# Cross-attention and rank-six self-attention on one core: second attention started inside the loop, additions shared out, unused TensorE products

## The chip, the core and the metric

The kernel runs on one core of a Trainium2 chip. The metric is the device time of one execution in microseconds (us). TensorE (PE) does the matrix products and the transposes, VectorE (DVE), ScalarE (ACT) and GpSimd (POOL) work on 128 partitions, SyncE (SP) issues all DMAs. SBUF tiles are named in the code; PSUM has eight banks of 128 x 512 fp32.

## What is computed

Two layers follow each other. B = 32 batches, N = 256 tokens, D = 256 features.

```python
# layer 0, 16 heads of 16 features; only the attention of batch 0 is used, and it is added to every batch
q, k, v = tgt @ Wq.T, memory @ Wk.T, memory @ Wv.T
x = tgt + softmax(q k^T / 4) v [batch 0]
# layer 1, per batch; ctx are the keys and values, x the queries
norm_X   = layernorm(ctx, norm1);  norm_F = layernorm(x, norm2)
attended = softmax(norm_F norm_X^T / 16) norm_X
h        = gelu(attended @ fc1_w.T + fc1_b)          # 4 hidden values per token
cross    = h @ fc2_w.T + fc2_b
norm_c   = layernorm(cross, norm3)
self_att = softmax(norm_c norm_c^T / 16) norm_c      # "second attention"
out      = norm_F + gamma2 * (cross + gamma1 * self_att)
```

Since `cross` is an affine function of 4 hidden values, `norm_c` has rank 6. The second attention therefore works on 6 numbers per token (`u` on one side, `uK` on the other), each cut into bf16 pieces so that the products keep fp32 accuracy.

## The kernel before

All engines run programs written out by hand, in which semaphores order the work between them; each engine works strictly in the order of its own program. There are four parts.

**First stage (layer 0, batch 0).** TensorE projects q, k and v (L822, L834). The 16 heads go through as eight pairs, `p` = 0 to 7: scores (L865), maxima on DVE (`hmax`, L380), exp on ACT (L718), transposes of the weights (L881) into banks 5 and 6, their copies to `PT` by ACT (bank 5, L724) and DVE (bank 6, L386), and after every other pair the product with v (L894). ACT's order per pair is four exps, then the copy of the pair ahead; TensorE's transposes wait for both copies (`pt0_ok`). DVE also takes statistics of ctx in between (L351), at `p` = 6 it clears the padding of `sU` (L400), and at `p` = 7 makes pieces of the output operand. The result is `tgt2`.

**Filling.** `tgt2` is added to `x`: batches 0 and 1 on DVE (L468), all others on POOL (`add`, L615). Then come statistics (L351), the root on POOL (L622), the normalising (DVE `normal`, L371 for x, POOL L635 for ctx), transposes on TensorE (L852) and their evacuation by ACT to `XT` and `Fall` (L735, L738), with weight and bias applied.

**The loop, b = 0 to 35.** TensorE per batch: the transposes of a later pair (L852), the scores (L915), and the transposes of the exps of the batch ahead (L923); once per four batches (a "quad", `q`) the hidden projection and its way back (L935, L943), the product of the weights with it (L953) and its way back (L961). DVE takes the maxima (`maximum`, L488), statistics and normals of later batches, and copies `vT` (L514) and `oTq` (L522); ACT does exps (L762) and the copies to `PT` (L756). The tables LATE and NEXT say behind which step DVE does which part of the small-rank algebra (`algebra(g, part)`, g = 0 for the first half of the batches, 1 for the second): h, gelu on ACT (`hidden`), the norm by Newton steps, `u`, `uK`, the pieces in `sU`. POOL makes the other side's pieces (`right`).

**Second attention and output, after the loop.** Sixteen pairs of batches, `p` = 0 to 15: transposes of `sU` into bank 4 (`turn`, L1001), their copy to `sT` (ACT for even, DVE for odd `p`), scores (L1012, into banks 0 and 1 or 2 and 3), maxima on DVE (`maxima`, L535), turned by TensorE (L1023), copied by ACT (`nm2T`, L781) and added to the scores by a product (`shift`, L1031), exp on ACT (L787). Per quad: the product with `u` (`attend`, L1044), a copy by DVE (`collected`, L548), the turn back (`back`, L1053), the division on DVE (`returned`, L553 to L558), pieces on POOL (`output_cuts`, L681 to L688), their transposes (`output_turn`, L1063, bank 4 too), ACT's copy to `cT` (L794). Per pair n: the output product (`output(n)`, L1073, banks 6 and 7) and the addition of `Fall` on DVE (`finish`, L564), after which SP stores the pair. `output(n)` comes five steps behind pair n and waits for `finish(n-1)`.

```python
        def output(n):
            pe.wait_ge(cT_ok, n // 2 + 1)
            if n >= 1:
                pe.wait_ge(fin_ok, n)
```

Of the kernel before, what the change touches and what calls it, by code (L numbers as in the profile page):

```python
# [28 lines left out]
P = 128  # L29
B = 32  # L30
# [17 lines left out]
LATE = {26: (0,), 29: (1,), 30: (2,), 31: (3,), 32: (4,), 33: (5,)}  # L48
NEXT = {0: (0,), 2: (1,), 3: (2, 3), 4: (4,), 5: (5,)}
# [21 lines left out]
def build(nc, x, ctx, x0t, c0t, wqt, wkt, wvt, params, out):  # L71
# [121 lines left out]
    h_ok, co_ok, sC_ok = sem("h_ok"), sem("co_ok"), sem("sC_ok")  # L193
# [44 lines left out]

    TURNS = [(p, 0) for p in range(EARLY)] + [(p, 1) for p in range(EARLY)] \
# [15 lines left out]
    def _(sp):  # L255
# [18 lines left out]
    def _(dve):  # L274
# [10 lines left out]
        def left_cuts(v, left, to, w):  # L285

            link(dve.tensor_copy(slots(to, w, SLOTS_L[0]), repeated(v, 3)))
            link(dve.tensor_tensor(left, v, to[:, :, 0:w], ALU.subtract))
            link(dve.tensor_copy(slots(to, w, SLOTS_L[1]), repeated(left, 2)))
            link(dve.tensor_tensor(to[:, :, 5 * w:6 * w], left, to[:, :, 3 * w:4 * w], ALU.subtract))  # L290

# [8 lines left out]

        dve.wait_ge(par_in, 16)
# [32 lines left out]
        output_operand(1)  # L334
# [5 lines left out]
        link(dve.tensor_copy(K[:, :], bank[5][:, 64:64 + U * U]), "QK")  # L340
        stats = [0]

        def statistics(b, side):
# [3 lines left out]
            elif b < 2:  # L347
                dve.wait_ge(y_first, b + 1)
            else:
                dve.wait_ge(y_ok, b - 1)  # L350
# [23 lines left out]
        for p in range(NHP + 1):  # L374
# [12 lines left out]
            if p < NHP:  # L387
# [32 lines left out]

        def products(v, m, n):

            w = big[:, 0:GROUP * n * n].rearrange("p (t j i) -> p t j i", t=GROUP, j=n)
            link(dve.tensor_tensor(w, v.unsqueeze(2).to_broadcast([P, GROUP, n, n]),
                                   m.rearrange("p (j i) -> p j i", j=n).unsqueeze(1).to_broadcast([P, GROUP, n, n]),
                                   ALU.mult))
            return w
# [6 lines left out]
        def algebra(g, part):  # L434
# [9 lines left out]
            elif part == 1:  # L444
                dve.wait_ge(gelu_ok, g + 1)
                dve.wait_ge(zero_ok, 8)
                link(dve.tensor_reduce(w5, products(ha[:, G, :], Q[:, :], H + 1), AX.X, ALU.add))
                link(dve.tensor_tensor(w5, w5, ha[:, G, :], ALU.mult))
                link(dve.tensor_reduce(v, w5, AX.X, ALU.add))
            elif part == 2:  # L450
# [4 lines left out]
            elif part == 3:  # L455
# [3 lines left out]
            elif part == 4:  # L459
# [692 lines left out]
```

## Time and profile before

| | |
|---|---|
| median of 3 runs (lowest to highest) | 263.16 us (262.43 to 263.74) |
| the profiled execution | 262.2 us, span 260.4 us |
| busy in the span | PE 213.0, DVE 207.4, ACT 140.9, POOL 125.4 us |
| granted TensorE clock, mean | 0.854 of full |

The page gives the busy share of each engine in forty slices of 6.5 us, the granted clock of TensorE in tenths, and groups of instructions by line. A timeline lists the instructions of one engine in order: start, length, engine, line, operation, count, and in brackets the idle time before them with what ended it. The chain of waits follows the last instruction back through whatever released it.

### The profile page before, as it was taken

What the parts mean: (1) busy time and instruction counts of PE and PEld (TensorE: products, weight loads), DVE (VectorE), ACT (ScalarE), POOL (GpSimd) and SP (SyncE); (2) the same over time, 40 slices, a digit from 0 to 9 for tenths busy, and PEclk for the clock granted to TensorE, in tenths of its full rate; (3) what the DMA queues carried; (4) which work ended last, traced back from release to release, by engine and by line L of the source; (5) the groups of instructions that cost most, each with busy time, mean ns of one, the idle gap of its engine ahead of it and who ended that gap; (6) DMA issues with size and microseconds to landing.
All of it is one profiled execution on the core that took longest, in us unless ns stands there. A gap on an engine that the chain in (4) does not pass through costs nothing.

```text
span 260.4 us, 4676 instructions
## 1 busy us (share of the span) xinstructions
PE 213.0 (82%) x1614; PEld 143.4 (55%) x1614; DVE 207.4 (80%) x413; ACT 140.9 (54%) x260; POOL 125.4 (48%) x186
## 2 busy tenths in 40 slices
PE   3989868289999999999999999963786568888731
PEld 3856535267778778796988789632222223333210
DVE  5678886999999989888998953886569958988663
ACT  1066764216677778586776778840564335454300
POOL 6000087677999979999697840041003512222220
PEclk9999999659999999999999999985555557777865
DMA  5980000044444425355450000000000024333556
GB/s 185 363 302 3 1 1 3 0 161 161 165 161 142 144 95 156 114 164 162 159 166 0 4 0 3 0 0 3 1 0 1 0 83 162 141 144 125 204 198 242
DMA packets 14711, 26.80 MB, mean 103 GB/s; under 512 B 1760, under 2 KB 1760, under 8 KB 14688
## 3 DMA queue, kind: packets, MB, share of 16 engines
q1 hardware_dynamic: 14688, 26.50, 29.2%
q8 instruction: 13, 0.21, 0.3%
q14 instruction: 10, 0.08, 0.1%
HBM read 18.11 MB, written 8.39 MB: 102 GB/s over the span
## 4 chain that ended last, share of the span: by engine, by line
PE 59%; DVE 24%; ACT 6%; issue 6%; POOL 2%; DMA 1%; SPq 0%; POOLq 0%; DVEq 0%; ACTq 0%
PE psum L915 17%; PE psum L852 8%; PE psum L923 5%; PE psum L1044 4%; DVE xN L371 4%; DVE nm L535 3%; DVE bn L351 3%; PE psum L953 3%; PE psum L822 2%; PE psum L935 2%; PE psum L1012 2%; DVE Fall L564 2%; PE psum L1073 2%; PE psum L865 2%; PE psum L881 2%
## 5 line engine op out<-in xcount | busy, mean ns | idle before, releaser
L915 PE MATMUL psum<-XT,Fall 128*128 128x256 f32 x256 | 62.6, 388 | 1.1 <-ACT Fall L738 1.1
L915 PEld LDWEIGHTS psum<-XT,Fall 128*128 128x128 f32 x256 | 47.2, 195 | 7.1 <-ACT Fall L738 1.7
L615 POOL TENSOR_TENSOR xN<-xN,tgt 128x512 f32<-128x512 f32 x30 | 39.1, 1306 | 1.5 <-DVE tgt L415 1.5
L635 POOL TENSOR_SCALAR cN<-cN,nmean,rstd 128x256 f32<-128x256 f32 x64 | 36.4, 579 | 2.4 <-POOL rstd L622 2.3
L371 DVE TENSOR_SCALAR xN<-xN,bn,rstd 128x256 f32<-128x256 f32 x64 | 34.8, 586 | 1.1 <-POOL rstd L622 1.1
L756 ACT ACTIVATE PT<-psum 128x512 f32<-128x512 f32 x32 | 19.1, 598 | 28.6 <-PE psum L923 28.6
L488 DVE TENSOR_REDUCE nmax<-psum 128x2 f32<-128x512 f32 x32 | 21.9, 684 | 12.6 <-PE psum L915 12.4
L622 POOL TENSOR_TENSOR rstd<-vps,minus_half 128x8 f32<-128x8 f32 (+1 forms) x16 | 24.8, 1549 | 13.8 <-DVE vps L362 13.8
L762 ACT ACTIVATE E<-psum,nmax 128x256 f32<-128x256 f32 x64 | 26.7, 473 | 8.3 <-DVE nmax L488 8.2
L681 POOL CAST sC<-co 128x160 bf16<-128x160 f32 x8 | 2.5, 317 | 53.9 <-DVE co L558 53.9
L738 ACT ACTIVATE Fall<-psum,par 128x512 f32<-128x512 f32 x32 | 23.4, 792 | 4.8 <-PE psum L852 4.7
L564 DVE TENSOR_TENSOR Fall<-psum,Fall 128x1024 f32<-128x1024 f32 x16 | 19.5, 1221 | 7.6 <-PE psum L1073 7.6
L735 ACT ACTIVATE XT<-psum,b1s,w1s 128x512 f32<-128x512 f32 x32 | 23.0, 788 | 3.7 <-PE psum L852 3.7
L535 DVE TENSOR_REDUCE nm<-psum 128x4 bf16<-128x1024 f32 x16 | 19.5, 1218 | 4.5 <-PE psum L1012 4.3
L351 DVE BATCH_NORM_STATS2 bn<-cN 128x6 f32<-128x512 f32 x32 | 22.2, 693 | 0.0
L852 PE MATMUL psum<-ident,xN 128*128 128x128 f32 x128 | 18.2, 289 | 4.7 <-DVE xN L371 4.7
L351 DVE BATCH_NORM_STATS2 bn<-xN 128x6 f32<-128x512 f32 x32 | 21.9, 685 | 0.0
L923 PE MATMUL psum<-ident,E 128*128 128x128 f32 x128 | 20.2, 280 | 1.6 <-ACT E L762 1.6
L787 ACT ACTIVATE PT<-psum 128x1024 f32<-128x1024 f32 x16 | 16.4, 1022 | 9.2 <-PE psum L1031 9.1
L923 PEld LDWEIGHTS psum<-ident,E 128*128 128x128 f32 x128 | 14.3, 141 | 9.6 <-issue 6.5
L852 PEld LDWEIGHTS psum<-ident,xN 128*128 128x128 f32 x128 | 15.7, 150 | 5.5 <-issue 5.1
L852 PE MATMUL psum<-ident,cN 128*128 128x128 f32 x128 | 17.1, 274 | 0.1
(156 smaller groups left out, 337.0 us busy)
## 6 DMA issues: line engine op xcount, KB each, us to landing
cN<-ctx SPq DMA_DIRECT2D x32, 256.0 KB, 2.9
xN<-x SPq DMA_DIRECT2D x32, 256.0 KB, 4.1
out<-Fall SPq DMA_DIRECT2D x32, 256.0 KB, 2.3
x0T<-x0t SPq DMA_DIRECT2D x1, 256.0 KB, 2.7
wqT<-wqt SPq DMA_DIRECT2D x1, 256.0 KB, 3.3
c0T<-c0t SPq DMA_DIRECT2D x1, 256.0 KB, 4.0
wkT<-wkt SPq DMA_DIRECT2D x1, 256.0 KB, 5.0
wvT<-wvt SPq DMA_DIRECT2D x1, 256.0 KB, 5.2
```

Source lines behind the costliest of these rows:

```text
L351: dve.bn_stats(bn[:, (b // 2) % 4, side, b % 2, :], src[:, b % SLOTS, :].rearrange("p (t d) -> p d t", t=NT)).then_inc(st_ok, 1)
L371: dve.tensor_scalar(own, own, stat(p, 1, m, t, 1), root_of(p, 1, m, t), ALU.subtract, ALU.mult)\
L535: dve.tensor_reduce(nm2[:, p % 2, :, 0:NT], scored(p).rearrange("p (m t k) -> p m t k", m=2, t=NT), AX.X, ALU.max, negate=True).then_inc(m ...
L564: dve.tensor_tensor(own, psum[:, 6 * 512:8 * 512], own, ALU.add).then_inc(fin_ok, 1)
L615: pool.tensor_tensor(xN[:, b % SLOTS, :], xN[:, b % SLOTS, :], tgt2[:, :, :].rearrange("p t d -> p (t d)"), ALU.add).then_inc(y_ok, 1)
L622: pool.tensor_tensor(rstd[:, p % 4, sides, :].rearrange("p s k -> p (s k)"), vps[:, p % 4, sides, :].rearrange("p s k -> p (s k)"), minus_ ...
L635: pool.tensor_scalar(own, own, nmean[:, p % 4, NT * m + t:NT * m + t + 1], root_of(p, 0, m, t), ALU.add, ALU.mult)\
L738: act.activation(Fall[:, 2 * p:2 * p + 2, c, :], tiles(own), ACT.Identity, bias=c_("b2", c), scale=c_("w2", c)).then_inc(evac_ok, 1)
L762: act.activation(E[:, b % 2, t * N:(t + 1) * N], bank[SBANK1[b % 3]][:, t * N:(t + 1) * N], ACT.Exp, bias=nmax[:, b % 2, t:t + 1]).then_in ...
L852: last = pe.transpose(bank[TBANK[n % 3]][:, m * N + t * P:m * N + (t + 1) * P], z[:, (2 * p + m) % SLOTS, t * D + c * P:t * D + (c + 1) * ...
L915: last = pe.matmul(bank[SBANK1[b % 3]][:, t * N:(t + 1) * N], Fall[:, b, c, t * P:(t + 1) * P], XT[:, p % 4, c, m * N:(m + 1) * N], start= ...
L923: last = pe.transpose(bank[SBANK1[b % 3]][:, k * N + t * P:k * N + (t + 1) * P], E[:, b % 2, t * N + k * P:t * N + (k + 1) * P], ident[:, :])
```

## The change

- **First stage.** ACT copies the pair ahead between the two halves of its exps, and TensorE's transposes wait only for the copy of their own bank. The clearing of `sU` moves to DVE's first instructions, the second part of the output operand out to loop step 18, and the first part of it behind the copies of Q and K. DVE adds `tgt2` to batches 2 and 3, too, and POOL starts its additions at batch 4, behind DVE's first four normals.
- **Loop.** `vT` and `oTq` are copied by ACT. The algebra of the first half is cut into nine parts and done at steps 20 to 29 (gelu at 21). The transposes and scores of the second attention's first pair are issued at b = 30 and 31, inside the loop; the last quad's `apply` and `apply_back` follow inside step p = 0 of the second attention.
- **Second attention.** All `sT` copies are done by ACT. For n = 1, 3, ... 13 (ASIDE) ACT copies the output from PSUM to the old space of `XT` behind the exp, and POOL adds `Fall` there. `output(13)` and `output(15)` use banks that the scores have left.
- **Unused products.** `keep_busy(n, b)` issues n products of the identity with itself into bank b, which nothing reads: 7 at the start, 11 behind the transposes of ctx, 4 and 3 at the change from the loop, 5 per step p below 5 and 2 per step after.

The diff, cut to its core:

```diff
-LATE = {26: (0,), 29: (1,), 30: (2,), 31: (3,), 32: (4,), 33: (5,)}
-NEXT = {0: (0,), 2: (1,), 3: (2, 3), 4: (4,), 5: (5,)}
+LATE = {20: (0,), 22: (1,), 23: (2,), 24: (3,), 25: (4,), 26: (5,), 27: (6,), 28: (7,), 29: (8,)}
+NEXT = {0: (0,), 2: (1, 2), 3: (3, 4), 4: (5, 6), 5: (7, 8)}
+ASIDE = tuple(range(1, 14, 2))
...
@@ sync @@
-        for b in range(B):
-            sp.wait_ge(fin_ok, b // 2 + 1)
+        for n, b in ((n, b) for n in STORED for b in (2 * n, 2 * n + 1)):
+            if n in ASIDE:
+                sp.wait_ge(added_ok, ASIDE.index(n) + 1)
+            else:
+                sp.wait_ge(fin_ok, own_adds(n) + 1)
...
@@ vector @@
+        for side in range(2):
+            dve.memset(sU[:, side, :, SU:SLOT], 0.0).then_inc(pads_ok, 1)
...
-                if p == 2 * EARLY:
-                    for side in range(2):
-                        dve.memset(sU[:, side, :, SU:SLOT], 0.0).then_inc(zero_ok, 1)
-                elif p > 2 * EARLY:
-                    output_operand(2)
...
-        statistics(2, 1)
+        add(2)
+        add(3)
         normal(0)
         normal(1)
+        statistics(2, 1)
...
-                dve.tensor_copy(vT[:, :], bank[6][:, 0:N]).then_inc(vT_ok, 1)
...
-                    dve.tensor_copy(oTq[:, :], bank[7][:, 0:N]).then_inc(oTq_ok, 1)
...
-        def turned(p):
...
-            dve.tensor_copy(sT[:, 1, :], bank[4][:, 0:NT * P].bitcast(BF16)).then_inc(sT_ok[1], 1)
...
         maxima(0)
-        turned(1)
+        saved(QUADS - 1)
         for p in range(2 * QUADS + 5):
...
-            if p >= 5:
+            if p >= 5 and p - 5 not in ASIDE:
                 finish(p - 5)
...
@@ gpsimd @@
+        def add_aside(n):
+            pool.wait_ge(aside_ok, ASIDE.index(n) + 1)
+            pool.tensor_tensor(pair(n), aside(n), pair(n), ALU.add).then_inc(added_ok, 1)
...
                 output_cuts((p - 3) // 2)
+            if p - 5 in ASIDE:
+                add_aside(p - 5)
...
@@ scalar @@
+                if m == 0 and p >= 1:
+                    act.wait_ge(p0_mm, 2 * p - 1)
...
+                    act.activation(PT[:, 2 * ((p - 1) % 3), :], bank[5][:, :], ACT.Copy).then_inc(pt0_ok[0], 1)
...
+        def set_aside(n):
+            act.wait_ge(f_mm, n + 1)
...
+            act.activation(aside(n), results(n), ACT.Copy).then_inc(aside_ok, 1)
...
-            if p % 2 == 0 and p + 2 < PAIRS:
+            if p + 2 < PAIRS:
                 turned(p + 2)
             if p < PAIRS:
                 weights(p)
+            if p - 5 in ASIDE:
+                set_aside(p - 5)
...
@@ tensor @@
+        def keep_busy(n, b):
+            for _ in range(n):
+                pe.matmul(bank[b][:, 0:P], ident[:, :], ident[:, :], start=True, stop=True)
+
+        pe.wait_ge(consts, 4)
+        keep_busy(7, 4)
...
-                if p >= 2:
-                    pe.wait_ge(pt0_ok[0], p - 1)
-                    pe.wait_ge(pt0_ok[1], p - 1)
                 for m in range(2):
+                    if p >= 2:
+                        pe.wait_ge(pt0_ok[m], p - 1)
...
+        keep_busy(11, 7)
...
+            if b == 31:
+                scores(0)
+            if b == B:
+                pe.wait_ge(V1_ok, QUADS)
+                keep_busy(4, 6)
+            if b >= 1:
+                weights_turned(b - 1)
...
+            if b == 30:
+                turn(0)
+            if b == 31:
+                turn(1)
         for p in range(2 * QUADS + 5):
             if p < PAIRS:
                 maxima_turn(p)
+            if p == 0:
+                keep_busy(3, 6)
+                apply(QUADS - 1)
             if p + 1 < PAIRS:
                 scores(p + 1)
+            if p == 0:
+                apply_back(QUADS - 1)
             if p + 2 < PAIRS:
                 turn(p + 2)
             if p < PAIRS:
                 shift(p)
+                keep_busy(5 if p < 5 else 2, 5)
```

TensorE's order from the last scores but one of the loop (L915, after the change L981) to the second attention, before and after. `stR` is the output operand, `E` the exps, `V` the hidden values, `sU` and `sT` the pieces of the second attention, `nm` its maxima.

```order
L915 MATMUL psum<-XT,Fall 128x256 x4
L961 MATMUL psum<-ident,oTq 128x128 x2
L923 MATMUL psum<-ident,E 128x128 x8
L953 MATMUL psum<-PT,V 5x256 x8
L961 MATMUL psum<-ident,oTq 128x128 x2
L1001 MATMUL psum<-identb,sU 128x128 x4
L1012 MATMUL psum<-sT 128x256 x4
L1001 MATMUL psum<-identb,sU 128x128 x4
L1023 MATMUL psum<-identb,nm 64x128
```

```order
L1048 MATMUL psum<-identb,sU 128x128 x4
L981 MATMUL psum<-XT,Fall 128x256 x4
L1027 MATMUL psum<-ident,oTq 128x128 x2
L1063 MATMUL psum<-sT 128x256 x4
L989 MATMUL psum<-ident,E 128x128 x4
L1048 MATMUL psum<-identb,sU 128x128 x4
L873 MATMUL psum<-ident 128x128 x4
L989 MATMUL psum<-ident,E 128x128 x4
L1074 MATMUL psum<-identb,nm 64x128
L873 MATMUL psum<-ident 128x128 x3
L1019 MATMUL psum<-PT,V 5x256 x8
```

The first `turn` (L1001, now L1048) has moved ahead of the last scores, the second attention's first scores (L1012, now L1063) directly behind them, and the last quad's product (L953, now L1019) behind the first turned maxima.

ACT's order in two steps p of the second attention, before and after (`PT` with 1024 columns is the exp of a pair, `XT` with 1024 columns the output set aside).

```order
L781 ACTIVATE nm2T<-psum 64x128
L775 ACTIVATE sT<-psum 128x512
L787 ACTIVATE PT<-psum 128x1024
L794 ACTIVATE cT<-psum 128x512
L781 ACTIVATE nm2T<-psum 64x128
L787 ACTIVATE PT<-psum 128x1024
```

```order
L830 ACTIVATE nm2T<-psum 64x128
L800 ACTIVATE sT<-psum 128x512
L838 ACTIVATE PT<-psum 128x1024
L851 ACTIVATE XT<-psum 128x1024
L845 ACTIVATE cT<-psum 128x512
L830 ACTIVATE nm2T<-psum 64x128
L800 ACTIVATE sT<-psum 128x512
L838 ACTIVATE PT<-psum 128x1024
```

Between the exp of an even step and the copy to `cT` stands the output set aside (L851), and odd steps have an `sT` copy.

## Rows read from the trace of the kernel before

**Rows 1.** The page: busy time by engine, and TensorE's granted clock by slice.

```profile
PE 213.0 (82%) x1614; PEld 143.4 (55%) x1614; DVE 207.4 (80%) x413; ACT 140.9 (54%) x260; POOL 125.4 (48%) x186
...
PEclk9999999659999999999999999985555557777865
```

**Rows 2.** Stretches: busy time of PE, PEld, DVE, ACT, POOL (last: PE alone), PEclk, DMA share, GB/s.

```profile
62.00:170.00 108.00, 107.48 (x825) 87.09 (x825) 92.40 (x201) 79.15 (x148) 80.04 (x88) 1.00 0.31 101
...
214.24:221.24 7.00, 6.25 (x58) 2.54 (x56) 5.89 (x9) 3.67 (x7) 1.50 (x5) 0.74 0.40 151
...
176.00:214.00 38.00, 24.56 (x173) 0.50 0.04 15
```

**Rows 3.** Timeline of TensorE, the first two projections.

```profile
4.92 3.78 PE L822 MATMUL psum<-x0T,wqT 128*128 128x256 f32 x8 [0.47 <-DMA wqT<-wqt]
8.50 2.88 PE L822 MATMUL psum<-c0T,wkT 128*128 128x256 f32 x8
```

**Rows 4.** Chain of waits in the first stage: start, length, what.

```profile
24.23 1.09 PE psum L865 x8
...
28.17 1.09 PE psum L881 x8
...
30.27 1.09 PE psum L865 x8
...
33.55 0.81 DVE sU L400
...
37.44 0.50 ACT PT L724
37.98 1.10 PE psum L881 x8
```

**Rows 5.** Filling: all x normals (least, median, most ns); their chain; TensorE's timeline.

```profile
L371 DVE TENSOR_SCALAR xN<-xN,bn,rstd x64: 396/404/1412, 48.7 to 157.8; 128x256 f32<-128x256 f32 x64
...
48.71 2.31 DVE xN L371 x4
...
52.97 3.27 DVE xN L371 x4
...
50.52 2.09 PE L852 MATMUL psum<-ident,xN 128*128 128x128 f32 x8 [4.69 <-DVE xN L371]
```

**Rows 6.** Timeline of ACT in the loop, around the gelu.

```profile
161.77 1.28 ACT L743 ACT_TABLE_LOAD   x1
```

**Rows 7.** Timelines of TensorE and DVE from the last loop scores to the first maxima.

```profile
168.49 1.95 PE L915 MATMUL psum<-XT,Fall 128*128 128x256 f32 x8
...
173.85 1.47 PE L953 MATMUL psum<-PT,V 128*5 128x256 f32 x16 [0.69 <-ACT PT L756]
178.32 0.69 PE L961 MATMUL psum<-ident,oTq 128*128 128x128 f32 x2 [2.99 <-DVE oTq L522]
...
180.77 1.23 DVE L535 TENSOR_REDUCE nm<-psum 128x4 bf16<-128x1024 f32 x1 [1.53 <-PE psum L1012]
```

**Rows 8.** Second attention: timelines of DVE, TensorE and ACT, then groups (busy, mean ns).

```profile
210.21 1.22 DVE L535 TENSOR_REDUCE nm<-psum 128x4 bf16<-128x1024 f32 x1
...
217.29 0.22 PE L1023 MATMUL psum<-identb,nm 128*64 128x128 bf16 x1 [0.74 <-DVE OB L553]
...
238.46 0.22 PE L1023 MATMUL psum<-identb,nm 128*64 128x128 bf16 x1 [1.03 <-DVE OB L553]
...
220.81 0.60 ACT L794 ACTIVATE cT<-psum 128x512 bf16<-128x512 bf16 x1 [1.02 <-PE psum L1063]
...
L787 ACT ACTIVATE PT<-psum 128x1024 f32<-128x1024 f32 x16 | 16.4, 1022 | 9.2 <-PE psum L1031 9.1
L564 DVE TENSOR_TENSOR Fall<-psum,Fall 128x1024 f32<-128x1024 f32 x16 | 19.5, 1221 | 7.6 <-PE psum L1073 7.6
L615 POOL TENSOR_TENSOR xN<-xN,tgt 128x512 f32<-128x512 f32 x30 | 39.1, 1306 | 1.5 <-DVE tgt L415 1.5
```

**Rows 9.** Timeline of DVE: the last addition.

```profile
256.02 1.23 DVE L564 TENSOR_TENSOR Fall<-psum,Fall 128x1024 f32<-128x1024 f32 x1 [0.80 <-PE psum L1073]
```

More of the change, by code:

```diff
@@ L237, in score_bank, with own_adds, result, results @@
         return bank[2 * (1 - p % 2) + m]
+    def own_adds(n):
+        return sum(i not in ASIDE for i in range(n))
+    STORED = tuple(range(13)) + (14, 13, 15)
+    def result(n):
+        return {13: (2, 3), 15: (0, 1)}.get(n, (6, 7))
+    def results(n):
+        a, _ = result(n)
+        return psum[:, 512 * a:512 * (a + 2)]
+    def aside(n):
+        return XT[:, (n // 2) % 2, :, :].rearrange("p c n -> p (c n)")
+    def pair(n):
+        return Fall[:, 2 * n:2 * n + 2, :, :].rearrange("p b c n -> p (b c n)")
     TURNS = [(p, 0) for p in range(EARLY)] + [(p, 1) for p in range(EARLY)] \
@@ L458, in algebra, with add @@
                 link(dve.tensor_tensor(u[:, G, 0:H + 1], ha[:, G, :], spread(y, H + 1), ALU.mult), ("u", g))
[L459 to L460 removed]
+            elif part == 5:
+                products(u[:, G, :], K[:, :], U)
+            elif part == 6:
+                link(dve.tensor_reduce(uK[:, G, :], produced(U), AX.X, ALU.add))
+            elif part == 7:
+                left_cut(uK[:, G, :], cut[:, G, 0:U], sU[:, 0, G, :], U)
             else:
[L462 removed]
+                left_rest(cut[:, G, 0:U], sU[:, 0, G, :], U)
                 ALG["left", g] = count[0]
[L465 removed]
+        def add(b):
             dve.wait_ge(tgt2_ok, 2 * NT)
@@ L499, in values, with saved @@
             dve.tensor_copy(V1[:, q % 2, :, :, 0:H], by_batch(bank[6][:, 0:N], H)).then_inc(V1_ok, 1)
-        for b in range(B + 4):
+        def saved(q):
+            dve.wait_ge(ob_mm, q + 1)
+            dve.tensor_copy(OA[:, q, :, :, :], by_batch(bank[7][:, 0:N], H + 1)).then_inc(o_saved, 1)
+        for b in range(B):
             k, m, q = b // 2, b % 2, b // 4
@@ L707, in _ @@
         for p in range(NHP + 1):
-            if p == 6:
-                act.wait_ge(o0_mm, NHP // 4)
-                act.activation(oT[:, 0, :], bank[0][:, :], ACT.Copy).then_inc(oT_ok[0], 1)
-            if p < NHP:
-                for m in range(2):
+            for m in range(2):
+                if p < NHP:
                     act.wait_ge(max0_ok, 2 * p + m + 1)
@@ L774, in turned @@
                 act.wait_ge(s2_mm, p - 1)
-            act.activation(sT[:, 0, :], bank[4][:, 0:NT * P].bitcast(BF16), ACT.Copy).then_inc(sT_ok[0], 1)
+            act.activation(sT[:, p % 2, :], bank[4][:, 0:NT * P].bitcast(BF16), ACT.Copy).then_inc(sT_ok[p % 2], 1)
+        for p in range(EARLY):
+            evacuate(p, 0)
+        evacuate(0, 1)
+        for b in range(B):
+            k, m, q = b // 2, b % 2, b // 4
+            if k + 1 < PAIRS and (m == 1 or k + 1 >= EARLY):
+                evacuate(k + 1, m)
+            if b >= 1:
+                weights_copied(b - 1)
+            exponentials(b)
+            if b % 4 == 1:
+                turned_values(q)
+            if b % 4 == 2 and q >= 1:
+                applied(q - 1)
+            if b == 21:
+                hidden(0)
+            if b == 29:
+                act.wait_ge(r_mm, 1)
+                act.activation(RT[:, :], bank[4][:, 0:DC * P // 2].bitcast(BF16), ACT.Copy).then_inc(rt_ok, 1)
+            if b == 30:
+                turned(0)
+        weights_copied(B - 1)
+        turned(1)
         def maxima_turned(p):
```

214 lines of the change are left out of this document (107 added, 107 removed).

## The prediction

> **What bounds the kernel now.** The page comes first [rows 1]: TensorE is busy for 213.0 of 260.4 us and DVE for 207.4, so no single engine bounds the whole, and TensorE's granted clock sags at the filling and in the last third. The stretches say which part has which limit [rows 2]. From 62 to 170 us TensorE is busy for 107.48 of 108 us at full clock: the loop is bound by TensorE, nothing can be taken from it by helping another engine, and any lateness of another engine adds to it. In one quad of the second attention (214.24 to 221.24) TensorE has 6.25 and DVE 5.89 of 7.00 us at a mean clock of 0.74: both are close to the limit, and TensorE's share shrinks if its clock rises. From 176 to 214 the clock is 0.50, that is 1.2 of 2.4 GHz, with TensorE busy for 24.56 of 38 us. Then the chain of waits and the timelines show the changes between parts: the start [rows 3], the first stage [rows 4], the filling [rows 5] and the 10.5 us between the end of the loop's last scores and the first maxima of the second attention [rows 7].
>
> All sums are made against the profiled execution, 262.2 us (span 260.4 and 1.8 around it), which lies 1.0 below the median of 263.16; the forecast adds that 1.0 back.
>
> **1. The start: -1.4.** The first projection takes 3.78 us for eight records and the second 2.88 [rows 3]; at full clock eight such records take some 1.9 (as L915 does in [rows 7], 1.95), so TensorE reached 2.4 GHz only about 4.5 us after the first projection began. Seven unused products start as soon as the identity is there. Each is worth half an L915 product, 0.22 us at full and 0.43 at half clock, so they fill about 3 us up to the first projection, which may start some 0.5 later. Nothing lost to half clock would be -2.8, less the 0.5 is -2.3; nothing gained and the late start is +0.5. I take -1.4, nearer the first, since the warm-up begins 3 us sooner.
>
> **2. First stage: -4.2.** Two head pairs take 6.0 us now, from scores to scores (24.23 to 30.27), and the chain runs through ACT's copy, then the transposes [rows 4]. With the copy between the halves of the exps, the transposes of bank 5 start 0.7 to 0.8 us earlier, before the second half, and TensorE becomes the limit: scores twice, transposes twice (1.1 each, less overlap) and the product with v (1.0) are 5.2. That is -0.8 in each of two such turns, -1.6. At the end the two memsets (0.81 and as much again) lie on the chain and leave it, -1.7; at the last pair the copy (0.50 at 37.44) stood behind both exp halves, and its transposes (37.98) now start one half and the copy earlier, -0.9. Together -4.2. The bounds are -1.7 (the memsets alone) and -6. The moved memsets cost nothing: they run before the parameters arrive. The pieces of the output operand now stand between the copies of Q and K and the first maxima, where DVE waits for the first scores anyway; without that cover they cost 0.8.
>
> **3. Filling: -2.0.** DVE is the chain here. Four normals take 2.31 and 3.27 us while POOL adds beside them, and one alone takes 0.40, four 1.6 [rows 5]. POOL's additions now wait for the first four: -0.7 there, and about -1.0 at the next four, which meet one addition instead of two. DVE's own two further additions (0.7 each when alone) run while POOL takes the root, where DVE has nothing else to do. With the `vT` copy moved to ACT (-0.3) this gives -2.0. The eleven products keep TensorE going through part of its 4.69 us of waiting; if its clock stays up, the first x transposes take 0.9 instead of 2.09 [rows 5] and the first scores 1.9 less, but DVE is not there earlier, so I book nothing for it. Bounds: 0 (POOL is simply late elsewhere) and -4. The contention itself shows in the least and the most of one normal, 396 and 1412 ns [rows 5]. The Trainium skill says in "SBUF — State Buffer" (§ SBUF: two separate sides) that DVE and GpSimd share one port pair, held for a whole instruction; by that rule the 3.27 would fall to 1.6 only where no addition starts between normals, and the trace agrees in kind.
>
> **4. Loop: +1.3.** TensorE has no slack, so what is moved in costs. The turn of the first pair adds 0.35. DVE has 15.6 us of idle time in 108 [rows 2], 0.5 per batch, and gains 0.2 by the two copies that go to ACT. Steps 20 to 25 bring 1.0 to 1.9 us each of algebra, while it still takes statistics. I let it fall behind by at most 2.5 us where the exp allows it about 1.2 to 2.2, so TensorE waits some 0.6. The gelu's two table loads at 21 (1.28 each [rows 6]) hold ACT by 2.9 us where evacuations still follow: 0.4. ACT is at 79 of 108 us, and two copies more per quad do not bound it. Bounds 0.35 and +4.
>
> **5. From the loop to the seventh `maxima`: -8.5.** Count from the end of the last loop scores, S. Now S is at 170.3 (last scores from 168.49, [rows 7]); the first maxima start 10.5 later, because `oTq` stands behind the algebra on DVE and the turn behind both [rows 7]; `maxima(7)` starts at 210.21, S + 39.9 [rows 8]. After: scores follow S directly (0.8), maxima(0) until 2.0; the last exps, four unused products, their transposes until 3.4; ACT's `PT` copy until 4.0; the last `apply` 4.3 to 5.3; scores of pair 1, `apply_back`, `saved` on DVE, so maxima(1) from 6.2. The lead of 9.7 shrinks there to 6.1. Then exp(0) ends at 8.0, maxima(2) runs from 8.5, maxima(3) from 10.8; the gelu's two table loads put exp(2) at 15. From 15 to 31 DVE is the limit with the algebra of the second half (about 9 us), maxima 4 to 6 and one `finish`; without its two `sT` copies and the stall behind the half-clock `attend` it reaches maxima(7) at S + 31.4. The difference is 8.5. The unused products, five per step, lie before work that waits for DVE. Bounds -5 and -11.
>
> **6. From there to step 14: -1.1.** Now 210.21 to 238.46 [rows 8], 28.2 us. DVE loses a `finish` (1.22, [rows 8]) and an `sT` copy per quad and would need only 4.5 us. But a new chain appears. ACT sets the output aside only when TensorE has ended an even step, 3.35 us of work at full clock; the copy takes 1.02 as an exp of equal size does, `cT` follows (0.60), and only then may the next `turn` overwrite bank 4 and `nm2T` be copied, whereupon turn, shift, two unused products, `back` and `output` take another 1.9. That is 3.35 + 1.6 + 1.9 = 6.9 per quad against 7.0 now. What remains is the start: 27.1 instead of 28.2. This hangs on full clock, and a range follows below. Bounds without the clock: -7 (period 5.5, TensorE's own work) and +1.
>
> **7. The end: +2.0.** From `mt` of step 14 (L1023, 238.46) to the end of the last addition (257.25) [rows 8, 9] are 18.8 us. After, POOL adds pair 11 before it makes the last pieces. A POOL addition of 512 columns takes 1.31 us [rows 8], of 1024 I take 2.5; it ends 2 us after the pieces could start. The last pieces, `cT` behind the set-aside of pair 13, and two additions in a row on free banks bring 19.75, +1.0; three pairs are stored together at the end, +1.0. The Trainium skill ("GPSIMD Engine Reference", § 3.1) measures 4.5 us for a GpSimd addition of 2048 fp32 and advises DVE for such work; that speaks against this part, and an estimate from it is 2.25 for 1024, 0.25 less than by the rows.
>
> **Sum.** -1.4 - 4.2 - 2.0 + 1.3 - 8.5 - 1.1 + 2.0 = -13.9, so 248.3 for an execution like the profiled one and **249.2** for the median.
>
> **The clock.** At 214 to 242 us it goes back and forth between 1.2 and 2.4 GHz (mean 0.74, [rows 2]), and it falls after stretches in which TensorE waited no longer than 0.74 to 1.03 us at a time [rows 8]. After, TensorE waits 1.15 of 6.9 us, with 0.9 us of full-width products more. I take it that those keep it up. "TensorE: Matmul & The Clock Gate" of the Trainium skill (§ HAM oscillation) names only long idle gaps between bursts as what throttles the array; by that rule the clock would stay up, and the sum above stands as it is. The rows disagree with it, and by them the next case is open.
>
> **Rivals.**
> - **The clock keeps swinging in the second attention.** With 5.2 us of TensorE work on the chain of a quad and about half the time at 1.2 GHz, T = 1.65 + 5.2 + T/4, near 8.5 to 9. At 8.5 against 6.9 over 3.9 quads that is +6.3: **255.5**. For it: [rows 2]. Against it: more and wider products.
> - **ACT and POOL take the additions without a hand-over cost**, since the copy falls into the time before the exp: the quad falls to 5.5, TensorE's own work, 1.4 less by 3.9 quads: **243.7**. For it: DVE's 5.89 of 7.00 is then gone. Against it: the order on ACT.
> - **The loop cannot feed the early start.** DVE's algebra or ACT's table loads make TensorE wait for 4 to 5 us around steps 21 to 26: **253.5**.
> - **The unused products do not lift the clock, which stays at 1.2 GHz as from 176 to 214 us [rows 2], and they then cost**: the 5.25 us of TensorE's work per quad become about 8.8 (a part of it does not follow the clock), with 1.6 that is 10.4; +3.5 by 3.9 is +13.7, and five products of 0.43 instead of 0.22 in each of three early steps on the chain are another +3.3: **266**, slower than before. It decides from a loss of 14 on, that is, when practically no stretch is at full clock. For it: 38 us at 0.50 with TensorE busy 65%. Against it: at 6.25 of 7.00 us busy [rows 2] it came back up each time.
>
> **How the numbers follow.** Forecast 0.59; swinging clock 0.17; no hand-over cost 0.15; loop late 0.05; low clock throughout 0.04. The forecast's own bounds (start, filling and stage each off by 1 to 2, mostly independent) make it 245 to 253. From 243 to 256 all cases but the last are in, less the tails of two, about 0.8. A change under 0.5%, 1.3 us, is about what can't be told from none. Faster 0.95, same 0.01, slower 0.04.
>
> **What would show it.** Right: `tgt2` ready near 38 us; L915's successor at 3.7 us per batch with waits under 1.5 us in all; first maxima 0.8 us behind the last scores and the second about 5 later; a quad near 6.9 us with a wait of about 1.1 us of TensorE for `cT`; PEclk 9 in the last third; `output_cuts(7)` behind POOL's addition. Wrong: quads near 5.5 or 8.5; PEclk of 5 to 7 behind 165 us; DVE maxima late in the loop from step 22; a first stage that still takes 6 us per two pairs.

## The result and the profile after

The changed kernel takes **269.92 us** (median of 4 runs, 267.93 to 270.31) against 263.45 (262.43 to 263.82) for the kernel before: ratio 1.0237, 95% interval 1.0176 to 1.0297. It is slower by 6.5 us. The forecast was 249.2, with a range of 243 to 256, so the result lies outside it, and on the other side of no change. The profiled execution takes 270.31 us, with a span of 268.5. Medians here and below are of all executions of a kernel, while ratios and their intervals leave out those more than 1.5% above its fastest, all of them at a lower granted clock (two of the four of e4, one of e11 with 258.64 us, among others).

The page of the changed kernel (busy time by engine, TensorE's granted clock in forty slices of 6.7 us, two of its groups):

```profile
span 268.5 us, 4992 instructions
...
PE 232.3 (87%) x1758; PEld 161.4 (60%) x1758; DVE 190.3 (71%) x384; ACT 155.4 (58%) x291; POOL 141.0 (53%) x191
...
PEclk9999999999999999999999999999855575575555
...
L711 POOL TENSOR_TENSOR Fall<-XT,Fall 128x1024 f32<-128x1024 f32 x7 | 16.5, 2354 | 31.2 <-ACT XT L851 31.2
...
L873 PE MATMUL psum<-ident 128*128 128x128 f32 x144 | 27.4, 343 | 1.9 <-POOL ident L608 1.9
```

Against [rows 1], DVE has 17 us less to do and TensorE 19 us more. The clock now holds through the filling and far into the second attention, and then stays at 1.2 GHz for most of the last 75 us. The unused products (L873) alone are busy for 27.4 us.

Where the time went, by four marks of the program (all from the timelines; the quad is (step 14 - step 8) / 3, and the tail runs from step 14 to the end of the span):

| us | before | after | difference | forecast |
|---|---|---|---|---|
| last loop scores start | 168.49 | 165.68 | -2.8 | -6.3 |
| from there to `maxima(7)` | 41.72 | 33.89 | -7.8 | -8.5 |
| from there to step 14 (TensorE's turn of the maxima) | 28.25 | 40.17 | **+11.9** | -1.1 |
| tail | 21.94 | 28.76 | **+6.8** | +2.0 |
| span | 260.4 | 268.5 | +8.1 | -13.9 |

At `maxima(7)` (199.57 against 210.21 of [rows 8]) the changed kernel led by 10.6 us. All of that was lost before step 14, and the tail then added to it. Stretches of TensorE in the changed kernel (busy time, records, granted clock, DMA):

```profile
186.00:192.00 6.00, 3.81 (x43) 1.00 0.00 1
192.00:198.00 6.00, 4.85 (x28) 0.51 0.00 0
198.00:204.00 6.00, 4.36 (x32) 0.50 0.25 90
204.00:210.00 6.00, 5.09 (x33) 0.50 0.14 52
210.00:216.00 6.00, 6.00 (x44) 0.50 0.33 123
216.00:222.00 6.00, 4.86 (x39) 0.78 0.30 107
222.00:228.00 6.00, 5.09 (x40) 0.50 0.19 72
```

The clock falls at 192 us, behind a wait of 2.11 us for DVE's algebra. One quad of it in TensorE's timeline:

```profile
212.71 1.89 PE L1095 MATMUL psum<-PT,u 128*6 128x256 f32 x16
214.53 0.61 PE L1114 MATMUL psum<-identb,sC 128*128 128x128 bf16 x4
215.07 0.61 PE L1130 MATMUL psum<-cT,RT 60*128 60x256 bf16 x4
215.61 0.32 PE L1074 MATMUL psum<-identb,nm 128*64 128x128 bf16 x1
215.86 0.45 PE L1063 MATMUL psum<-sT 36*128 36x256 bf16 x4
217.38 0.38 PE L1048 MATMUL psum<-identb,sU 128*128 128x128 bf16 x4 [1.07 <-ACT cT L845]
217.69 0.39 PE L1082 MATMUL psum<-nm2T,sel 2*128 2x256 bf16 x4
218.01 0.71 PE L873 MATMUL psum<-ident 128*128 128x128 f32 x4
...
219.48 0.61 PE L1063 MATMUL psum<-sT 36*128 36x256 bf16 x4
220.02 0.61 PE L1048 MATMUL psum<-identb,sU 128*128 128x128 bf16 x4
220.56 0.61 PE L1082 MATMUL psum<-nm2T,sel 2*128 2x256 bf16 x4
221.10 1.22 PE L873 MATMUL psum<-ident 128*128 128x128 f32 x4
```

and what ACT does meanwhile:

```profile
211.67 1.02 ACT L838 ACTIVATE PT<-psum 128x1024 f32<-128x1024 f32 x1
215.72 1.02 ACT L851 ACTIVATE XT<-psum 128x1024 f32<-128x1024 f32 x1 [3.03 <-PE psum L1130]
216.64 0.59 ACT L845 ACTIVATE cT<-psum 128x512 bf16<-128x512 bf16 x1
```

The same shapes take 0.39 us at one level of the clock and 0.61 at the other. TensorE is busy for 6.00 of 6.00 us from 210 to 216, the clock comes back, TensorE waits 1.07 us for `cT`, and 2.1 us behind that wait it is at 1.2 GHz again. The source of `cT` (L1114) ends at 215.14, but its copy starts at 216.64: the copy set aside stands ahead of it in ACT's program and needs `output` (L1130), which TensorE does after L1114. So `cT` comes 1.5 us late, and ACT stood idle for 3.03 us before.

The chain of waits from 180 to 262 us shows who pays (shares of that stretch):

```profile
by line: PE psum L873 15.8%; PE psum L1095 12.4%; issue 11.4%; PE psum L1130 8.3%; PE psum L1082 7.3%; PE psum L1048 5.7%; PE psum L1114 4.8%; PE psum L1063 4.0%; ACT cT L845 3.6%; DVE nm L564 3.0%; POOL Fall L711 2.9%; PE psum L1104 2.6%; 
```

The unused products are the largest entry, 15.8% of 82 us, that is 13 us.

### The profile page after: what moved, and what is told of

Its sections match the earlier page's. It is cut to its first block, busy times and chain, and to the rows that moved or that the text cites. A ratio compares the mean times of both kernels' runs of the same rounds, so it can differ in the third digit from the quotient of the medians.

```text
span 268.5 us, 4992 instructions
## 1 busy us (share of the span) xinstructions
PE 232.3 (87%) x1758; PEld 161.4 (60%) x1758; DVE 190.3 (71%) x384; ACT 155.4 (58%) x291; POOL 141.0 (53%) x191
## 4 chain that ended last, share of the span: by engine, by line
PE 60%; DVE 21%; issue 7%; ACT 6%; POOL 3%; ACTq 1%; DVEq 0%; POOLq 0%
PE psum L981 14%; PE psum L873 7%; PE psum L918 6%; DVE bn L381 5%; DVE xN L401 5%; PE psum L989 5%; PE psum L1095 4%; PE psum L1019 3%; PE psum L1130 3%; PE psum L1082 2%; PE psum L1048 2%; PE psum L931 2%; DVE nmax L524 2%; PE psum L1001 2%; PE psum L888 2%
## 5 line engine op out<-in xcount | busy, mean ns | idle before, releaser
L981 PE MATMUL psum<-XT,Fall 128*128 128x256 f32 x256 | 60.9, 381 | 1.8 <-ACT Fall L763 1.8
L981 PEld LDWEIGHTS psum<-XT,Fall 128*128 128x128 f32 x256 | 46.1, 190 | 7.2 <-ACT Fall L763 2.2
L656 POOL TENSOR_SCALAR cN<-cN,nmean,rstd 128x256 f32<-128x256 f32 x64 | 38.8, 618 | 2.4 <-POOL rstd L643 2.3
L636 POOL TENSOR_TENSOR xN<-xN,tgt 128x512 f32<-128x512 f32 x28 | 35.7, 1278 | 1.6 <-DVE xN L401 1.6
L401 DVE TENSOR_SCALAR xN<-xN,bn,rstd 128x256 f32<-128x256 f32 x64 | 33.9, 573 | 0.7 <-POOL rstd L643 0.7
L711 POOL TENSOR_TENSOR Fall<-XT,Fall 128x1024 f32<-128x1024 f32 x7 | 16.5, 2354 | 31.2 <-ACT XT L851 31.2
L873 PE MATMUL psum<-ident 128*128 128x128 f32 x144 | 27.4, 343 | 1.9 <-POOL ident L608 1.9
L873 PEld LDWEIGHTS psum<-ident 128*128 128x128 f32 x144 | 22.7, 237 | 7.1 <-issue 5.2
L851 ACT ACTIVATE XT<-psum 128x1024 f32<-128x1024 f32 x7 | 7.2, 1024 | 24.3 <-PE psum L1130 24.3
L989 PE MATMUL psum<-ident,E 128*128 128x128 f32 x128 | 20.2, 280 | 0.3 <-ACT E L793 0.2
L918 PE MATMUL psum<-ident,xN 128*128 128x128 f32 x128 | 17.1, 274 | 2.6 <-DVE xN L401 2.3
L989 PEld LDWEIGHTS psum<-ident,E 128*128 128x128 f32 x128 | 14.3, 141 | 8.3 <-issue 6.3
```

The costliest lines, as they stand in the source:

```text
L401: dve.tensor_scalar(own, own, stat(p, 1, m, t, 1), root_of(p, 1, m, t), ALU.subtract, ALU.mult)\
L636: pool.tensor_tensor(xN[:, b % SLOTS, :], xN[:, b % SLOTS, :], tgt2[:, :, :].rearrange("p t d -> p (t d)"), ALU.add).then_inc(y_ok, 1)
L656: pool.tensor_scalar(own, own, nmean[:, p % 4, NT * m + t:NT * m + t + 1], root_of(p, 0, m, t), ALU.add, ALU.mult)\
L873: pe.matmul(bank[b][:, 0:P], ident[:, :], ident[:, :], start=True, stop=True)
L918: last = pe.transpose(bank[TBANK[n % 3]][:, m * N + t * P:m * N + (t + 1) * P], z[:, (2 * p + m) % SLOTS, t * D + c * P:t * D + (c + 1) * ...
L981: last = pe.matmul(bank[SBANK1[b % 3]][:, t * N:(t + 1) * N], Fall[:, b, c, t * P:(t + 1) * P], XT[:, p % 4, c, m * N:(m + 1) * N], start= ...
```

## The experiments

Theory A: the copy set aside ahead of `cT` makes TensorE wait; the waits bring the clock down and keep it there, and at that clock nearly all of TensorE's work is on the chain. Rival B: the unused products themselves are the cost. Rival C: they hold the clock up and are worth having. Rival D: the `sT` copies, all on ACT now, make the wait. "The kernel before" was run beside each group; its medians were 262.62, 263.45 and 263.63. What every profile showed, in us:

| kernel | median | clock | `maxima(7)` at | quad | tail |
|---|---|---|---|---|---|
| before | 263.45 | 0.854 | 210.21 | 7.06 | 21.94 |
| after | 269.92 | 0.870 | 199.57 | 10.02 | 28.76 |
| e1 no step products | 260.22 | 0.856 | 198.42 | 8.37 | 26.74 |
| e2 no aside | 247.93 | 0.951 | 199.08 | 6.15 | 20.37 |
| e3 `cT` first | 253.39 | 0.939 | 198.60 | 7.07 | 24.03 |
| e4 neither | 248.64 | 0.910 | 198.09 | 6.05 | 20.51 |
| e5 five everywhere | 269.75 | 0.934 | 198.49 | 9.52 | 27.6 |
| e6 e2, more products | 251.55 | 0.949 | 200.51 | 6.13 | 20.65 |
| e7 before + products | 269.93 | 0.876 | 216.20 | 6.46 | 23.15 |
| e8 e3, pieces first | 251.39 | 0.955 | 198.41 | 6.56 | 23.33 |
| e9 e2, algebra earlier | **244.03** | 0.964 | 197.31 | 6.13 | 20.3 |
| e10 e9, few products | 245.75 | 0.928 | 197.91 | 6.13 | 20.03 |
| e11 e2, none at the start | 248.81 | 0.936 | 200.30 | 6.13 | 20.33 |
| e12 e2, filling as before | 249.56 | 0.932 | 200.88 | 6.15 | 20.33 |

### Products and additions, each alone and together

e1 takes the products out of the steps, e2 the additions off ACT and POOL, e4 does both, e3 only exchanges two calls:

```diff
 e1, e4:
-                keep_busy(5 if p < 5 else 2, 5)
 e2, e4:
-ASIDE = tuple(range(1, 14, 2))
+ASIDE = ()
-    STORED = tuple(range(13)) + (14, 13, 15)
+    STORED = tuple(range(16))
 e3, ACT's program:
-            if p - 5 in ASIDE:
-                set_aside(p - 5)
             if p == 1:
                 hidden(1)
             if p % 2 == 0 and p >= 4:
                 output_turned((p - 4) // 2)
+            if p - 5 in ASIDE:
+                set_aside(p - 5)
```

> The changed kernel without the unused products of the second attention's steps (5, then 2 per step); those at the start, behind the transposes of ctx and at the change from the loop stay. Theory A (ACT's copy of the output ahead of cT makes TensorE wait, the waits lower the clock, the products cannot lift it): quads of 9 to 10 us still at 1.2 GHz, time 263 to 267, that is 3 to 7 less than the changed kernel's 269.9, since at half clock two products (about 1.1 us a pair of steps) and the five of each early step lie on the chain. Rival B (the products themselves are the cost): quads near 7, time 255 to 259. Rival C (the products do hold the clock up in part): no faster, 270 to 274, with a granted clock lower than now.

> The changed kernel with all additions on DVE as before and the pairs stored in order; everything else of the change stays, the unused products too. Theory A (the copy set aside on ACT between the exp and cT stretches the quad and so lowers the clock): quads of 7 to 7.5 us at a swinging clock, the lead of 10 us at the first turn of the second half is kept, and the end is near 19 us again: time 252 to 258. Rival B (the unused products lie on the chain at half clock): quads of 8 to 9, 261 to 266. Rival D (all sT copies on ACT make the wait): quads still over 10, time 268 to 271.

> The changed kernel with one thing moved: ACT copies cT ahead of the output that it sets aside, in every even step. Theory A: cT comes 1.0 us earlier, TensorE's wait of 0.9 to 1.1 us for it in each quad goes, quads fall from 10.4 to 9.4 at least, 5 quads: time 263 to 266, and 255 to 258 if the clock comes back. Rival B (products) or D (sT copies): 269 to 271, since the wait for cT is then only a sign.

> Both of the first two edits: all additions on DVE, no unused products in the steps of the second attention. Theory A: as without the copies set aside, 252 to 257, the products then lie in waits and cost under 1 us or hold the clock. Rival B: 250 to 254, at least 5 less than with the products. Rival C (products hold the clock): 3 or more longer than with the products.

Measured, as ratios to the kernel before: e1 0.9936 (0.9902 to 0.9971), e2 0.9477 (0.9402 to 0.9553), e3 0.9682 (0.9618 to 0.9746), e4 0.9412 (0.9305 to 0.9519).

- **e3 decides for A.** One exchange of calls on ACT, with no work removed, is worth 16.5 us (269.92 to 253.39). Before the run I put it at 4 to 7, or 12 to 15 if the clock comes back. It comes back, and the gain lies just above that range. Page and a quad of e3:

```profile
PEclk9999999799999999999999999999998589799955
```

```profile
206.76:213.30 6.54, 5.90 (x64) 3.11 (x65) 4.81 (x8) 4.96 (x8) 3.86 (x7) 1.00 0.43 160
```

```profile
209.94 0.60 ACT L845 ACTIVATE cT<-psum 128x512 bf16<-128x512 bf16 x1 [0.76 <-PE psum L1114]
210.44 1.02 ACT L851 ACTIVATE XT<-psum 128x1024 f32<-128x1024 f32 x1
211.34 0.26 ACT L830 ACTIVATE nm2T<-psum 64x128 bf16<-64x128 bf16 x1
```

The copy of `cT` starts right behind L1114 (209.51, 0.40 long), not 1.5 us later. TensorE's longest wait in the quad falls from 1.07 to 0.58 us (now for `nm2T`), and the quad is 6.54 us long. At full clock the quad of the changed kernel would be some 6.8 us (an estimate from e5, below), so the wait itself is a small part of the difference to 10.02 and the clock is the rest.

- **e2** comes out 4 us below A's 252 to 258. It has quads of 6.12 us at full clock, with TensorE busy for 5.82 and DVE for 5.56 (stretch 210.44 to 216.56):

```profile
210.44:216.56 6.12, 5.82 (x66) 3.10 (x65) 5.56 (x8) 4.09 (x8) 1.51 (x5) 1.00 0.47 173
```

All 16 additions on DVE are thus no bound, and D falls, since the `sT` copies are still all on ACT. The early start of the second attention keeps its lead of 11 us. The clock of e2 falls too, around TensorE's waits of 2.10 and 1.72 us for DVE's algebra (which end at 191.92 and 196.02), but here it is back at 204.5 us and stays for the rest of the quads:

```profile
PEclk9999999889999999999999999999999858999965
```

- **The products** cost 9.7 us where the copy is set aside (e1, between A's 263 to 267 and B's 255 to 259), and nothing that can be told where it is not (e2 and e4 differ by 0.7; the executions of e4 run from 245.47 to 250.80, those of e2 from 247.56 to 248.30). B is therefore half right: they cost as long as the clock is low. C falls for these steps: without the products the quads of e4 are as short (6.05) at a lower mean clock. That two products per step take back what the full clock gives is argued from these two quads, not shown by itself. Both e2 and e4 lie below every range that I gave for them.

### Can more products bring the clock back?

```diff
 e5, after with:
-                keep_busy(5 if p < 5 else 2, 5)
+                keep_busy(5, 5)
 e6, e2 with:
+                keep_busy({5: 10, 6: 9}.get(p, 5 if p < 5 else 2), 5)
 e7, before with, behind shift(p):
+                keep_busy(5 if p < 5 else 2, 5)
 e8, e3 with, in POOL's program:
-            if p % 2 == 1 and 3 <= p < 2 * QUADS + 3:
+            if p % 2 == 1 and 3 <= p < 2 * QUADS + 1:
                 output_cuts((p - 3) // 2)
+            if p == 2 * QUADS:
+                output_cuts(QUADS - 1)
             if p - 5 in ASIDE:
                 add_aside(p - 5)
```

> The changed kernel with five unused products in every step of the second attention, not two behind the fifth. Theory A (TensorE's wait for cT pins the clock at 1.2 GHz, and no product stands in that wait, since each has its place behind the shift): six products more per quad at 0.55 us each at half clock are up to 3.3 us a quad, 5.5 quads: 280 to 288. Rival C (more products would lift the clock): quads near 7.5, time 252 to 260.

> The kernel with all additions on DVE (247.9 us) with ten instead of two unused products... in step 5 five more and in step 6 seven more than there, placed before the waits of 2.1 and 1.7 us for DVE's algebra, so that TensorE does not stand still there; everything else as in that kernel. Theory A (such waits throw the clock down, here from 196 to 204 us): granted clock full up to 199 us and time 245 to 248. If the clock falls all the same, behind the wait of 2.3 us for the turn, or the products lie on the chain: 248 to 251.

> The kernel before with one thing added: the unused products of the steps of the second attention (five per step below 5, two per step after). Theory A (products lift the clock only where they stand in TensorE's waits; before, it waits 0.74 to 1.03 us at a time for DVE): the clock of 176 to 214 us rises in part, the last third swings; 258 to 264. Rival B (products are a cost at half clock): 266 to 272. Rival C (products hold the clock): 252 to 257, mean clock over 0.93.

> The kernel in which cT is copied ahead of the output set aside (253.4 us), with POOL's last pieces of the output operand also made ahead of its addition of pair 11. If the addition ahead of the pieces is what the end lost: 2.0 to 2.4 us earlier, 250.8 to 251.6. If the last two additions on POOL, one behind the other and 2.35 each, set the end instead: 253 to 254.

There is no interval for these four; the medians beside the 263.45 of the kernel before are 269.75, 251.55, 269.93 and 251.39.

- **e5** was expected wrongly by both. The clock rises (0.919 to 0.934 in its four executions, 0.870 to 0.888 in those of the changed kernel), and the time is that of the changed kernel (267.17 to 270.81 against 267.93 to 270.31). A quad of it, at full clock throughout in spite of a wait of 1.16 us for `cT`:

```profile
224.90:233.35 8.45, 7.22 (x78) 4.47 (x77) 4.53 (x7) 4.96 (x8) 3.85 (x6) 1.00 0.27 96
```

```profile
226.60 0.38 PE L1048 MATMUL psum<-identb,sU 128*128 128x128 bf16 x4 [1.16 <-ACT cT L845]
```

Ten records, five products, take 1.38 us at full clock, so the six products that a quad has more than in the changed kernel are 1.65. Without them this quad would be 6.8 us long: an estimate, but it bears out my 6.9 for the chain at full clock, and puts the error on the clock. Over the whole kernel the six products cost about what the clock brings.

- **e7** is the plainest case against the products: 6.5 us more on the kernel before, though its clock is higher (0.876) and its last quads shorter (6.46 against 7.06). That is rival B's range. The loss is made earlier: `maxima(7)` comes 6.0 later, because the five products of each early step lie on the chain of waits at half clock, where they take 2.43 us each time (2.50 with their overlap):

```profile
183.49 2.50 PE L813 MATMUL psum<-ident 128*128 128x128 f32 x10
```

- **e6** is 3.6 slower than e2, just above the second of its ranges. The products do not hold the clock, which falls at about 194 us, and 18 records of them then take 4.21 us at half clock, ahead of `attend`, which DVE waits for:

```profile
200.58 0.58 PE L1048 MATMUL psum<-identb,sU 128*128 128x128 bf16 x4 [2.59 <-issue]
201.09 0.61 PE L1082 MATMUL psum<-nm2T,sel 2*128 2x256 bf16 x4
201.63 4.21 PE L873 MATMUL psum<-ident 128*128 128x128 f32 x18
```

- **e8** is 2.0 us below e3, as its first expectation had it, but only 0.7 of that is in the tail (24.03 to 23.33), where the edit acts. The rest lies ahead of it, in quads that caught more of the full clock (6.56 against 7.07). So its time fits the first expectation, but its tail fits the rival: the last two additions on POOL, 4.74 us in a row, set the end:

```profile
238.25 0.33 POOL L707 TENSOR_TENSOR sC<-cut,sC 128x80 bf16<-128x80 f32 x1
238.54 4.74 POOL L711 TENSOR_TENSOR Fall<-XT,Fall 128x1024 f32<-128x1024 f32 x2
```

Products inside the wait for `cT` itself were not tried: bank 5 holds the turned maxima there, which ACT has still to read, and the other banks hold scores and results in use.

### The remaining waits, the start and the filling

```diff
 e9, e2 with:
-NEXT = {0: (0,), 2: (1, 2), 3: (3, 4), 4: (5, 6), 5: (7, 8)}
+NEXT = {0: (0,), 1: (1, 2), 2: (3, 4), 3: (5, 6), 4: (7, 8)}
 e10, e9 with:
+                keep_busy(0 if p < 5 else 2, 5)
 e11, e2 without:
-        keep_busy(7, 4)
-        keep_busy(11, 7)
 e12, e2 with POOL adding batches 2 and 3 again:
-        add(2)
-        add(3)
         normal(0)
...
-                pool.wait_ge(zy_ok, 4)
...
+        add(2)
+        add(3)
         root(0)
```

> All additions on DVE (the 247.9 us kernel), and the algebra of the second half of the batches one step earlier: parts 1 and 2 behind the third maxima (p = 1), where DVE stands idle for 2.7 us, 3 and 4 at p = 2, 5 and 6 at 3, 7 and 8 at 4. Theory A (TensorE's waits of 2.1, 1.7 and 2.3 us for this algebra at 189 to 199 us throw the clock down and are themselves lost): 2 to 3 us of the waits go, the clock falls later or not at all, another 1 to 3: 242 to 246. Rival: DVE is as late, since its work is the same and only shifted: 247 to 249.

> As the kernel with the earlier algebra, without the five products of each of the first five steps; the two per step behind them stay. Theory B (products are only a cost): the same or up to 1.5 less. Theory C (the early products keep the clock up until DVE's waits are over): 2 to 4 more, with the clock at half from 178 us on.

> All additions on DVE, without the seven unused products at the start and the eleven behind the transposes of ctx. By the traces, the first projections end 0.9 us earlier with them, and the transposes of x run at full clock: 0.9 to 2 us more without, 248.8 to 250. If the products there do nothing: 247 to 248.5.

> All additions on DVE, with the filling as it was before: tgt2 added to batches 2 and 3 by POOL, which does not wait for the first normals. My term of the prediction was 2.0 us for this; the traces show the first four normals at 1.38 (2.31 before) and the next four at 3.26 (3.27 before), with 1.3 us of DVE work more: 0 to 0.8 longer, 247.9 to 248.8. If the change of the split is worth its 2.0: 249.5 to 250.3.

Ratios to the kernel before: e9 0.9275 (0.9238 to 0.9311), e10 0.9324 (0.9284 to 0.9364), e11 0.9439 (0.9399 to 0.9478), e12 0.9473 (0.9442 to 0.9504).

- **e9** lies in A's range of 242 to 246 and gains 3.9 us on e2: 1.8 of it up to `maxima(7)`, and 1.7 at the next quad, where the clock now hardly falls.

```profile
PEclk9999999989999999999999999999999989999965
```

It is the fastest version, 26 us under the changed kernel and 19.6 under the one before.
- **e10** is 1.7 slower, near C's 2 to 4. At this place the early products hold the clock, since they stand where TensorE waits for DVE anyway; without them it is at half from 178 to 198 us (0.50 in each stretch of 4 us there), with them at full up to 194. So C is right for these five steps, though for less than it said, and wrong for the later ones.
- **e11** and **e12** size two terms, against e2: the products of start and filling 0.9 us (`maxima(7)` 1.2 later without them; the executions of the two kernels overlap, 248.06 to 249.14 and 247.56 to 248.30, so this is at the edge of what can be told), and the split of the filling 1.6 (`maxima(7)` 1.8 later). For the second I had expected 0 to 0.8; the rival, that it is worth its 2.0, had 249.5 to 250.3, where the 249.56 lies.

## Why the prediction was wrong

**Start and first stage (-1.4, -4.2): -3.8**, by the start of DVE's first addition of `tgt2` (40.03 against 43.78). Two head pairs take 5.66 us (22.89 to 28.55) instead of 6.0 [rows 4], not 5.2: TensorE is busy for 5.42 of them, but the chain still runs from the scores over DVE's maxima, ACT's exps and the copy between them (0.60) back to the transposes. The projections end 0.9 earlier (10.30 against 11.22), not 1.4.

**Filling (-2.0): -0.5 in the trace.** The new split alone is worth 1.6 (e12), so the filling would have lost 1.1 of the earlier `tgt2` without it; by what is not settled. The first four normals fell as forecast, the next four did not: two additions of POOL still run beside them (from 48.64 for 2.53 us; before, from 52.91), where I had counted one (timeline of DVE; the like in [rows 5] are 2.31 and 3.27):

```profile
44.72 1.38 DVE L401 TENSOR_SCALAR xN<-xN,bn,rstd 128x256 f32<-128x256 f32 x4 [0.31 <-POOL rstd L643]
...
48.70 3.26 DVE L401 TENSOR_SCALAR xN<-xN,bn,rstd 128x256 f32<-128x256 f32 x4 [0.42 <-POOL rstd L643]
```

The Trainium skill's rule of one shared port pair ("SBUF — State Buffer", § SBUF: two separate sides) agrees in kind with both: no addition runs beside the first four, two run beside the second.

By the end of these three terms the kernel led by 4.25 us (the L989 at 66.41 against L923 at 70.66) instead of 7.6.

**Loop (+1.3): right.** The lead falls from 4.25 to 2.8, with a wait of 0.91 us for `oTq` behind the table loads.

**From the loop to `maxima(7)` (-8.5): right**, -7.8.

**To step 14 (-1.1): the step that failed.** I wrote that the quad would be 6.9 us, that it "hangs on full clock", and that TensorE's wait of 1.15 us would be outweighed by the products: "I take it that those keep it up." It was 10.0. The chain of 6.9 is right at full clock (e5). The clock fell behind the waits for DVE's algebra at 192 us, whose effect on it I had not counted, and the wait for `cT`, once per quad, brought it down again each time it had come back. The low-clock rival had the outcome (quads at 1.2 GHz, which the products do not lift and on which they then cost) and the price (10.4 per quad, 266 us), though not the wait for `cT` as its cause, and got 0.04. Its sum was near the measured time partly by luck: it had 3.3 us for the products of the early steps, where the changed kernel lost 0.7 against the forecast, and nothing more for the end, where it lost 4.8. What I held against it, that the clock "came back up each time", was true of [rows 2, 8] at waits of 0.74 to 1.03 us and of swings, not of a stay at full clock; I read the swing as a sign that little was missing. The swinging rival was also solved wrongly: T = 1.65 + 5.2 + T/4 gives 9.1 us, not 8.5, and with it about 258 us, outside my range. The Trainium skill's account of how idle gaps throttle the array ("TensorE: Matmul & The Clock Gate", § HAM oscillation) speaks of long gaps; read as I read it, the clock would have stayed up behind waits of 1.07 us, and the trace of the changed kernel disagrees.

I also priced the hand-over as if it were given by the work. It came from the order of two calls on ACT, by which `cT` was copied 1.5 us after it could be. The rival without a hand-over cost had to be brought about by an exchange of calls (e3) or by leaving the copy out (e2). It gives 6.1 to 6.5 per quad, not 5.5: TensorE is then near its limit (busy for 5.82 of 6.12 us in e2, 5.90 of 6.54 in e3), and with all additions DVE too (5.56 of 6.12).

**The end (+2.0): +6.8.** The order was read rightly (the pieces behind POOL's addition), but at half clock, and ACT's copy stands ahead of `cT` once more. In e3, with the clock higher and `cT` first, the tail is 24.03, that is +2.1, about the +2.0 of the forecast. Timelines of TensorE, POOL and ACT in the changed kernel:

```profile
258.02 0.61 PE L1114 MATMUL psum<-identb,sC 128*128 128x128 bf16 x4 [3.06 <-POOL sC L707]
258.56 0.61 PE L1130 MATMUL psum<-cT,RT 60*128 60x256 bf16 x4
260.77 1.03 PE L1130 MATMUL psum<-cT,RT 60*128 60x256 bf16 x8 [1.61 <-ACT cT L845]
```

```profile
253.89 2.40 POOL L711 TENSOR_TENSOR Fall<-XT,Fall 128x1024 f32<-128x1024 f32 x1 [2.35 <-ACT XT L851]
256.23 0.32 POOL L700 CAST sC<-co 128x160 bf16<-128x160 f32 x1
```

```profile
259.21 1.02 ACT L851 ACTIVATE XT<-psum 128x1024 f32<-128x1024 f32 x1 [4.91 <-PE psum L1130]
260.13 0.59 ACT L845 ACTIVATE cT<-psum 128x512 bf16<-128x512 bf16 x1
```

Without the additions set aside the tail is 20.4 (e2), shorter than before: POOL's part was a loss here, not a gain.

**The unused products** were counted in the late steps only as two per quad at full clock, inside the 6.9, and as free before `maxima(7)`. They are 13 us of the chain from 180 to 262 us, and their removal gives 9.7 back, of which 1.15 lies ahead of `maxima(7)` (199.57 against 198.42).

Open: what exactly makes the clock fall. In e3 it fell once in the middle of the quads, in the one from 213.30 to 221.36, behind a wait of 0.58 us like those of the quads that kept it. e5 kept it full over a wait of 1.16 us for `cT`. And e9 kept it full through a stretch with a wait of 2.28 us, in which TensorE was busy for little more than half the time:

```profile
182.00:186.00 4.00, 2.72 (x25) 1.00 0.00 0
186.00:190.00 4.00, 2.29 (x23) 1.00 0.00 0
190.00:194.00 4.00, 3.09 (x39) 1.00 0.01 2
```

So no single wait is the switch. What is shown is that with the repeated wait for `cT` (after) the clock stays down for the most part, that with it shortened (e3) or gone (e2) the clock comes back and stays for the most part, and that more products lift it without a gain (e5, e7).

## What to carry to other kernels

Where an engine copies for another, put first what the bound engine waits for: compare when the source of the copy was ready with when the copy began. When a forecast hangs on a clock that swings in the trace, forecast at both levels, and do not give the lower one a small chance as long as a wait of about 1 us per period stays, as it did here. Fill TensorE's time with unused products only where a row shows it waiting; elsewhere they cost what they bring, and more at half clock.

## What the runs showed of the hardware

- More clock is not more speed: e5 has a granted clock of 0.919 to 0.934 against 0.870 to 0.888 and the same time; e4 has quads of 6.05 us at a swinging clock, e2 of 6.15 at full.
- In the changed kernel TensorE was busy for 6.00 of 6.00 us before the clock rose at 216 us; it fell again 2.1 us behind a wait of 1.07 us, and again 2.1 us behind one of 1.04 us at 237.78. In e5 and e9 it stayed full over waits of 1.16 and 2.28 us.
- A GpSimd addition of 128 x 1024 fp32 took 2354 ns, the same addition on DVE 1.22 us out of PSUM; an unused 128 x 128 fp32 product 0.26 to 0.28 us at full clock (five in 1.31 us, from 187.62 to 188.93 after) and 0.47 to 0.58 at half (nine in 4.21 in e6, five in 2.43 in e7, two in 1.15 after).
- The first four normals of the filling took 1.38 us with no GpSimd addition beside them, and four more of the same shape 3.26 us beside two (changed kernel, 44.72 and 48.70).
